# A graph network on one core: the widened tables of seven source tiles, interleaved or side by side

## The reference

```python
def _graph_conv(x, W, b, src, dst, norm_src, norm_dst, n_nodes, act):
    h = x @ W
    m = h[src] * norm_src[:, None]
    agg = jax.ops.segment_sum(m, dst, num_segments=n_nodes)
    out = agg * norm_dst[:, None] + b
    return jax.nn.relu(out) if act else out

h = _graph_conv(feats, W1, b1, src, dst, norm_src, norm_dst, n, act=True)
h = _graph_conv(h, W2, b2, src, dst, norm_src, norm_dst, n, act=True)
h = _graph_conv(h, W3, b3, src, dst, norm_src, norm_dst, n, act=False)
```

## Time and profile before

| what | us |
| --- | --- |
| median of three runs | 4062.52 (4061.83 to 4063.08) |
| span of the profiled execution | 4526.7 |
| preparation, in the profile | 0 to 835 |
| layers, in the profile | 835 to 2020 |
| edge stage and output, in the profile | 2020 to 4527 |
| TensorE busy over the span | 3408.9 (75%) |
| VectorE busy | 3296.3 (73%) |
| ScalarE busy | 2866.3 (63%) |

### The profile page before, as it was taken

How to read it: one execution, slowest core, us unless ns; L and a number is a source line. 1 busy time by engine, 2 the same in 40 slices (tenths; PEclk the granted TensorE clock), 3 DMA queues, 4 the chain that set the end, 5 groups by cost and what they waited for, 6 DMA issues and landing times. The chain is left out here.

```text
span 4526.7 us, 61194 instructions
## 1 busy us (share of the span) xinstructions
PE 3408.9 (75%) x21477; PEld 2773.7 (61%) x21477; DVE 3296.3 (73%) x5075; ACT 2866.3 (63%) x3090; POOL 1926.4 (43%) x1883
## 2 busy tenths in 40 slices
PE   5888889899999999965566666666666666666642
PEld 4777777688888888844445555555555555555542
DVE  9999999755555555545667777777777777777774
ACT  3666665544444454436667777777777777777753
POOL 6222000412102201135556666666666666666633
PEclk9888888899999999987777777877777777777775
DMA  4444333699999999964556666676666666666632
GB/s 139 130 131 132 128 127 128 242 308 305 304 302 307 305 301 313 319 194 134 141 157 182 175 179 178 176 182 176 180 177 176 181 177 180 175 178 179 174 112 59
DMA packets 363341, 876.56 MB, mean 194 GB/s; under 512 B 54730, under 2 KB 213695, under 8 KB 363175
## 3 DMA queue, kind: packets, MB, share of 16 engines
q1 hardware_dynamic: 272471, 739.80, 50.5%
q0 software_dynamic: 59936, 119.71, 13.4%
q10 hardware_dynamic: 30768, 15.26, 1.1%
HBM read 653.46 MB, written 221.09 MB: 193 GB/s over the span
## 5 line engine op out<-in xcount | busy, mean ns | idle before, releaser
L1198 POOL DMA_INDIRECT hgat<-x_rows,edge_src x1564 | 1475.6, 943 | 889.7 <-DVE prod_e L1361 451.9
L898 PE MATMUL psum<-wide,hp 128*128 128x490 f32 x4704 | 1096.2, 394 | 14.8 <-DVE wide L988 14.1
L898 PEld LDWEIGHTS psum<-wide,hp 128*128 128x128 f32 x4704 | 884.1, 189 | 208.0 <-issue 15.7
L821 ACT CAST wide<-gran 128x1470 fp32r<-128x1470 bf16 x336 | 478.1, 1423 | 582.1 <-PE psum L898 562.0
L1303 PE MATMUL psum<-c_b,one_b 96*128 96x512 bf16 x391 | 213.0, 545 | 794.7 <-ACT a L1247 742.0
L988 DVE CAST wide<-gran 128x1960 fp32r<-128x1960 bf16 x336 | 447.2, 1331 | 436.5 <-PE psum L898 403.5
L609 PEld LDWEIGHTS psum<-hi_hot,lo_hot 128*128 128x128 bf16 x7840 | 545.5, 155 | 215.7 <-issue 73.0
L1379 DVE TENSOR_SCALAR psum<-rows_e,edge_same,edge_first 128x128 f32<-128x128 f32 x1564 | 644.9, 412 | 42.5
L1307 PEld LDWEIGHTS psum<-v_sb,excess 128*128 128x128 f32 x3128 | 629.0, 280 | 36.5
L525 ACT CAST stage<-psum 128x490 bf16<-128x490 f32 x784 | 451.2, 576 | 306.4 <-PE psum L609 296.6
L609 PE MATMUL psum<-hi_hot,lo_hot 128*128 128x49 bf16 x7840 | 573.7, 219 | 91.7 <-DVE hi_hot L401 90.3
(11 more groups left out here) (218 smaller groups left out, 3655.5 us busy)
## 6 DMA issues: line engine op xcount, KB each, us to landing
gran<-step_counts SPq DMA_DIRECT2D x336, 857.5 KB
dist<-weight_by_step SPq DMA_DIRECT2D x195, 512.0 KB
running_products<-rows_e SPq DMA_DIRECT2D x195, 512.0 KB
step_counts<-stage SPq DMA_DIRECT2D x112, 857.5 KB
ef<-in_edge_attr SPq DMA_DIRECT2D x195, 448.0 KB
hgat<-x_rows,edge_src POOLq DMA_INDIRECT x1564
kn<-keep_and_norm_of_steps SPq DMA_DIRECT2D x48, 490.0 KB
ef<-in_edge_attr SPq DMA_DIRECT2D x171, 64.0 KB
```

The costliest lines, as they stand in the source:

```text
L821: nc.scalar.copy(wide[:, i % WIDE, :, NEARC:SB], gran[:, i % RING, :, NEARC:SB]).then_inc(s_wf, 1)
L898: last = nc.tensor.matmul(y, hps[:, 7 * g + t, part, :], wide[:, r, :, t * IS:(t + 1) * IS], start=first, stop=last_)
L1198: pool.indirect_dma_start(out=hgat[:, f % U, c, :], out_offset=None, in_=x1_d, in_offset=bass.IndirectOffsetOnAxis(ap=edge_src[:, 2 * f + ...
```

## The change

The slot of `wide` keeps its size, 7 x 490 numbers in each partition, but its outer index becomes the source tile and its inner one the step. The two casts regroup the numbers while they widen them: they read `gran` piece by piece of 70 in the order tile, stretch, step and write the tiles one behind the other. VectorE still writes tiles 0 to 3 and ScalarE 4 to 6. The matmul reads `wide[:, r, t, :]`. The loads, the waits and the counts of instructions stay as they are.

```diff
             gran = sbt("gran", [P, RING, 7, SB], BF16)
             wide = sbt("wide", [P, WIDE, 7, SB], F32R)
+            by_tile = lambda ring, i, a, b: ring[:, i % RING, :, a * IS:b * IS].rearrange("p i (t s) -> p t i s", s=IS)
+            in_runs = lambda i, a, b: wide[:, i % WIDE, a:b, 0:SB].rearrange("p t (i s) -> p t i s", s=IS)
@@ widen on ScalarE
-                            nc.scalar.copy(wide[:, i % WIDE, :, NEARC:SB], gran[:, i % RING, :, NEARC:SB]).then_inc(s_wf, 1)
+                            nc.scalar.copy(in_runs(i, NEAR, 7), by_tile(gran, i, NEAR, 7)).then_inc(s_wf, 1)
@@ granule on TensorE
-                                last = nc.tensor.matmul(y, hps[:, 7 * g + t, part, :], wide[:, r, :, t * IS:(t + 1) * IS],
+                                last = nc.tensor.matmul(y, hps[:, 7 * g + t, part, :], wide[:, r, t, :],
                                                         start=first, stop=last_)
@@ widen on VectorE
-                            nc.vector.tensor_copy(wide[:, i % WIDE, :, 0:NEARC], gran[:, i % RING, :, 0:NEARC]
-                                                  ).then_inc(s_wn, 1)
+                            nc.vector.tensor_copy(in_runs(i, 0, NEAR), by_tile(gran, i, 0, NEAR)).then_inc(s_wn, 1)
```

## The result

| kernel | median, us | ratio to before (95% interval) |
| --- | --- | --- |
| before | 4062.8 | |
| changed | 4029.3 | 0.9916 (0.9902 to 0.9930) |

The change gains 33.5 us where 99 were forecast. The time lies in the stated range (3943 to 4066), but not in that of the forecast (3943 to 3983): it is rival (B), which had a chance of 0.08 and stood at 3991 to 4048.

A forecast was written before the change was run, and what follows sets the result against it. TensorE was taken to bound the layers by the distance of their 4704 matmuls. Saving 21 ns each gives 0.294 us a granule, times 336 granules 99 us, with casts hidden: 4062.5 - 99 = 3964 us, range 3943 to 4066.

The forecast's parts named there:

- rival (B): Layers' matmul: runs cause only part of the remainder, 3 to 15 ns a matmul; 3991 to 4048 us; chance 0.08.
- cover: Widening casts of VectorE and ScalarE stay hidden behind TensorE, their idle 1.89 and 1.80 us a granule shrinking by 0.29.
- transfers: Loads of the ring must come 10% faster, 336 GB/s instead of 307, and still fit.
- layer change: Scaling at a layer change comes 2.9 us earlier; some 5 us remain for the last gather's landing.
- The step from the profiled span to the median: Whole kernel: the 99 us are subtracted unscaled from the median 4062.5, though the profiled span was 464 us longer.
- the pick of 21 ns in part 1: Layers' matmul reading one run instead of seven: 21 ns saved each, 0.294 us a granule, 99 us in all.
- (b): Line 560, 490 bf16 columns in 49 runs: next matmul after 0.23 us, as behind line 898's seven 4-byte runs.
- (a): Line 1303, 512 adjacent bf16 columns, 0.22 us apart: 210.5 ns for 490 columns, saving 19 ns.
- (c): Shortest durations of lines 898, 560 and 1303: one run of 490 would have 367 ns, so breaks cost 20 to 23.
- (d): Line 1292, 512 adjacent 4-byte columns in two passes: 0.43 us apart, two whole clocks a column without a remainder.
- (A): Layers' matmul: remainder belongs to 4-byte one-pass data or something else than the seven runs; no gain, 4062 us; chance 0.19.
- (C): VectorE's cast pays at each of 28 short runs and becomes the limit; 91 us more, 4153 us; chance 0.07.

The follow-up runs named there:

- 384 columns: Changed kernel, each matmul except a block's first moving only the first 384 of 490 columns: 3911.3 us; the same with ring rows 512 numbers apart: 3920.9 us.
- 49 runs: Changed kernel's casts, with each matmul reading 49 runs of ten, 70 apart, instead of one run of 490: 4282.4 us.
- the bf16 run: Changed kernel with both operands of the layers' matmul in bf16, the moving data still one run: 3962.6 us.
- rows 512 apart: Changed kernel with rows of the widened ring 512 numbers apart instead of 490: 4019.2 us; with both matmul operands also in bf16: 3958.7 us.
- Half the weights: Changed kernel, every matmul except a block's first and last loading 64 of the 128 weight columns: 4025.5 us.

## Why the prediction was wrong

**Bound, cover, transfers, layer change: right.** The layers followed the distance of the matmuls. ScalarE's cast stayed at 1.43 us (1.42 taken), VectorE's went to 1.18 (1.2 taken, between 1.05 and 2.36), and TensorE waited for neither between 900 and 1900 us. The loads rose to 318 GB/s and kept up; even 357 with 384 columns were fed. The gathers' margin held for TensorE: VectorE waited for gathered rows once, 3.9 us, and TensorE not behind it; with the 7.6 us of the 384 columns it was spent. The step from the profiled span to the median was right as well.

**The failed step is the pick of 21 ns in part 1.** The ends, 0 and 25 ns, held; 7.3 lay between them. That the excess shows at the full clock alone, which the prediction took for a limit of what feeds the array, is borne out by the 49 runs at the low clock; that nearly all of it belongs to the breaks is not. The four neighbours were each read for more than they showed:

- (b) said that two broken patterns of unlike types take the same 230 ns, and took this as a sign of a common price for being broken. It was chance: 48 breaks at 0.47 ns and six at 1.2 ns, on top of unlike distances without a break (207.4 and 222.4). Dividing by the number of breaks would have shown it: 25 ns over bare columns are 0.5 ns a break in line 560 and 4 in line 898, and nothing in the argument said why a break between runs of 280 bytes should cost eight times as much.
- (a) and (c) used line 1303, which moves bf16. The 367 ns that (c) worked out for one run came true to the nanosecond, in the bf16 run; for the 4-byte type it is 378.
- (d) was the only 4-byte neighbour, and its two clocks a column leave room for a price that shows at one clock a column. The 0.439 ns a column measured here lie below its 0.83 and above the 0.417 of this matmul. It could not speak about the pace in question. The earlier trace rows would have said the same: at the low clock a column lasts 0.83 ns, and nothing was left over.

The 25.5 ns over bare columns that each matmul had before can be split so: 7.3 for six breaks, 2.4 for starts of rows 490 apart, and 16 that remain with one run and rows 512 apart. Of these bf16 has 2.5 too (206.7 - 204.2). By the two widths the 16 are (0.439 - 0.417) x 490 = 11 for 4-byte columns and 5 a matmul, which is an estimate, as said above.

**The rivals.** (B) came true in size. Of its mechanism, more memory touched at the ends of runs, only the price by the number of runs is shown, not how it arises. (A), that the remainder belongs to the 4-byte type, is true of over half of it (222.4 - 207.4 = 15 of 25.5 ns). I gave it 0.19 only as an alternative to the forecast; a split of the 25 ns between both was the case to weigh most. (C) did not happen: the short runs cost VectorE nothing, as the row with runs of ten had said.

**On the two rules.** The Trainium skill's rule on hops between runs ("Vector Engine (DVE) Microarchitecture Reference", section 5.2), carried over to TensorE, would have made the gain 0. On TensorE a hop isn't free at the clock of 1.00: 1.2 ns in 4-byte data, 0.47 in 2-byte data. Read as an addition, the 60 cycles a matmul of the Trainium skill's "TensorEngine Tiling (Array Packing)", Instruction Overhead, would by estimate give (490 + 60) / 2.4 = 229 ns for any of these matmuls of 490 columns. Bf16 with one run has 207.4.

**Still open.** Why a 4-byte column takes some 5% more than a clock isn't shown, nor how a break comes to cost what it does. Half the weights changed the distance by 0.7 ns, the casts by nothing. The price of a break is counted from rows 490 apart, whose starts cost something too; counted from rows 512 apart it would be (229.7 - 220.0) / 6 = 1.6 and (277.2 - 220.0) / 48 = 1.2 ns. 4-byte weights with 2-byte moving data were not tried, so a share of the weights' type in what 4-byte data has over bf16 is not ruled out.

## What to carry to other kernels

When the distance of matmuls is longer than their columns, split the excess before pricing a cure: so much a break, so much a column of this type, so much a matmul, and ask of each neighbouring row which of these it contains. A neighbour of another type, or at another pace, bounds a price but doesn't set it; two equal totals aren't a common cause until they have been divided by what differs between them. Here the type was worth more than the layout, where the precision allows it: 90 us with seven runs (4062.8 - 3972.7) and 67 with one, against the 33 of the layout, 100 together.

## What the runs showed of the hardware

- A break in the moving data costs TensorE 1.1 to 1.2 ns in 4-byte and 0.47 ns in 2-byte data at the granted clock of 1.00. At 0.50 the 48 breaks of 49 runs cost nothing (0.408 us for 490 columns).
- 4-byte one-pass columns with 4-byte weights take 0.439 ns at the clock of 1.00 by the two widths run, 0.417 being the clock; rows that start 1960 bytes apart cost another 2.4 ns a matmul over rows 2048 bytes apart (222.4 against 220.0).
- VectorE's cast became 0.15 us faster with an outer count of 4 instead of 7: 1.33 to 1.18 us for the same 1960 elements, although the runs that it reads became shorter. Writing to bf16 it is 0.68 us with 4 and 0.75 with 7. No run changed the outer count alone, but writing four runs 512 apart instead of one left it at 1.18. The Trainium skill ("Vector Engine (DVE) Microarchitecture Reference", section 5.1) has the first of two ports take the larger half of an odd outer count. Four rows of 280 against half of 1960 are 140 elements more, and by estimate 0.147 us / 140 = 1.05 ns an element, which the 1.08 us for 896 elements (1.2 ns with all that is fixed) doesn't contradict.
- TensorE lost nothing to casts on the same ring that ran 0.8 us beside each us of its own work, VectorE's and ScalarE's added (365.3 + 439.4 of 1000 us): 222.4 ns with them, 222.5 with casts of two numbers a tile.
